# Spreading a kernel's indirect transfers: one lookup or redirection fewer in passes that also gather source rows

## The reference, cut to what matters

```
h  = relu(x @ W_self0 + mean(x[src] by dst) @ W_neigh0 + b0)
h  = h @ W_self1 + mean(h[src] by dst) @ W_neigh1 + b1
x1 = layernorm(x + h)
q = x1@Wq+bq;  k = x1@Wk+bk;  v = x1@Wv+bv;  e = edge_attr@We+be      (4 heads of 128)
alpha = q[dst].(k[src]+e) / sqrt(128);  attn = softmax of alpha by dst
out = sum by dst of (v[src]+e)*attn + x1@Wskip+bskip
z   = elu(layernorm(out) @ Wlin + blin + x1)
result = layernorm(x1 + z)
```

## Time and profile before

| | us |
|---|---|
| median of three runs | 1648.03 |
| profiled execution, its own time | 1646.39 |
| its span | 1644.6 |
| node stage, windows 41 to 650 | 609.0, PE busy 576.5, DVE 595.0, ACT 565.3, POOL 489.9 |
| first sampling stage, windows 650 to 812 | 162.0, PE busy 145.8, DVE 96.6, ACT 59.9, POOL 84.4 |
| second sampling stage, windows 812 to 965 | 153.0, PE busy 141.1, POOL 98.2 |
| edge stage, windows 965 to 1645 | 680.0, PE busy 614.8 |

### The profile page before, as it was taken

One profiled execution on the slowest core, in us unless ns is written; L12 is line 12 of the kernel. 1 busy time (PEld: TensorE's weight loads), 2 busy tenths in 40 slices (PEclk: granted clock), 3 DMA queues, 4 the chain that ended last, 5 costly groups with the idle time before them and its releaser, 6 DMA issues. The chain is left out here.

```text
span 1644.6 us, 33984 instructions
## 1 busy us (share of the span) xinstructions
PE 1495.9 (91%) x7847; PEld 1041.7 (63%) x7847; DVE 1292.1 (79%) x6158; ACT 1179.7 (72%) x3174; POOL 1030.3 (63%) x1038
## 2 busy tenths in 40 slices
PE   4999999999999997999699967999999999999972
PEld 3777777777777775888566643555555555555541
DVE  5999999999999998666468754777777777777762
ACT  2999999999999997344257742777777777777772
POOL 2888888868888884676167627455565555565320
PEclk9999999999999999999899989999999999999996
DMA  2567666644444443233179853333333333333210
GB/s 78 143 161 158 157 159 159 158 149 147 147 147 149 147 147 110 73 94 94 48 225 291 283 180 96 82 82 90 88 90 88 89 88 84 88 89 90 62 37 5
DMA packets 156184, 199.53 MB, mean 121 GB/s; under 512 B 36159, under 2 KB 79342, under 8 KB 156070
## 3 DMA queue, kind: packets, MB, share of 16 engines
q1 hardware_dynamic: 127450, 160.43, 32.4%
q0 software_dynamic: 27200, 36.26, 10.2%
q10 hardware_dynamic: 1420, 1.60, 0.3%
HBM read 106.66 MB, written 100.07 MB: 126 GB/s over the span
## 5 line engine op out<-in xcount | busy, mean ns | idle before, releaser
L1377 POOL DMA_INDIRECT big<-x_tab,look x196 | 199.5, 1018 | 91.7 <-issue 36.9
L1394 POOL DMA_INDIRECT out_dram<-big,idx x98 | 99.8, 1018 | 223.2 <-PE pb L1432 147.8
L737 PE MATMUL pb<-MG_s,big 128*128 128x256 f32 x832 | 207.4, 392 | 26.5 <-ACT big L770 26.4
L737 PEld LDWEIGHTS pb<-MG_s,big 128*128 128x128 f32 x832 | 149.5, 189 | 128.5 <-ACT big L770 112.3
L746 ACT ACTIVATE big<-big 128x128 f32<-128x128 f32 x416 | 180.3, 482 | 0.0
L1611 DVE CUSTOM_DVE_ANT_0 big<-pb,big,zero 128x128 f32<-128x128 f32 x392 | 120.2, 347 | 69.5 <-PE pb L1470 69.3
L719 PE MATMUL pb<-C_s,big 128*128 128x128 f32 x832 | 161.4, 276 | 0.0
L720 PE MATMUL pb<-Ws1c_s,big 128*128 128x128 f32 x832 | 161.3, 276 | 0.0
L868 POOL TENSOR_TENSOR big<-big,cl 128x512 f32<-128x512 f32 x104 | 133.7, 1285 | 36.7 <-DVE big L842 35.7
L1108 POOL DMA_INDIRECT big<-h1e_tab,hidx x98 | 98.2, 1002 | 75.0 <-POOLq L1829 34.1
L1481 PEld LDWEIGHTS pb<-Wg_s,big 128*128 128x128 f32 x784 | 103.1, 192 | 47.3 <-issue 43.8
(11 more groups left out here) (354 smaller groups left out, 4003.1 us busy)
## 6 DMA issues: line engine op xcount, KB each, us to landing
big<-in_x_dram SPq DMA_DIRECT2D x104, 256.0 KB
x_tab<-big SPq DMA_DIRECT2D x98, 256.0 KB
out_dram<-big SPq DMA_DIRECT2D x98, 256.0 KB, 2.2
c_ve<-ve_tab SPq DMA_DIRECT2D x98, 256.0 KB, 2.8
ve_tab<-c_ve SPq DMA_DIRECT2D x66, 256.0 KB
h1e_tab<-a_rows SPq DMA_DIRECT2D x25, 256.0 KB, 2.6
x_tab<-a_rows SPq DMA_DIRECT2D x25, 256.0 KB, 3.7
big<-in_edge_attr_dram SPq DMA_DIRECT2D x97, 64.0 KB
```

The costliest lines, as they stand in the source:

```text
L737: t = pe.matmul(o, b_x1T[:, r * P:(r + 1) * P], MG_s[:], start=True, stop=True)
L1377: g.indirect_dma_start(out=o, out_offset=None, in_=x1_tab, in_offset=bass.IndirectOffsetOnAxis(ap=look[:, a, j:j + 1], axis=0), bounds_che ...
```

## The change

A pass with a `gather_src` has one slot where the others have two, so every pass that also has a `node_row` issues at most three indirect transfers. The 16 slots given up shift the later ones back. Redirections now end in pass 53 (before: pass 49). The first lookup is at slot `NT` + 3 = 101, in pass 55 (before: slot 104, pass 52). 91 lookups fit up to pass 103. The other seven are issued in the first sampling stage, behind POOL's last `gather_src`, and the waits for the lookups and the four operations that make `hidx` go there with them. `after`, `run_matrices`, `a_pool` and others are only moved in the file, to stand behind `b_pool`; this part of the diff is left out.

```diff
+        LOOK_AT = NT + 3
+        B_LOOKS = 2 * TILES - 4 * R - LOOK_AT
+        assert 0 < B_LOOKS < NT and TILES >= 6 * 4 * R
+
+        def look_up(g, e):
+
+            g.indirect_dma_start(out=look[:, 0, e:e + 1], out_offset=None, in_=redirect,
+                                 in_offset=bass.IndirectOffsetOnAxis(ap=idx[:, SRC, e:e + 1], axis=0),
+                                 bounds_check=N - 1, oob_is_err=False).then_inc(dma_k[e % 4], 16)
...
-                if it % 6 == 5 and it < 96:
+                brings = it % 6 == 5 and it < 6 * 4 * R
+                if brings:
                     gather_src(g, it // 6 // R, it // 6 % R)
-                for t in range(2 * it, 2 * it + 2):
+                slot = 2 * it - min(it // 6, 4 * R)
+                for t in range(slot, slot + (1 if brings else 2)):
                     if t < NT:
                         redirect_rows(idx[:, REP, t:t + 1], idx[:, EID, t:t + 1], t % 4)
                     elif t == NT:
                         redirect_rows(split_i[:], tail_i[:, 1:2], t % 4)
-                    elif t >= TILES and t - TILES < NT:
-                        if t == TILES:
+                    elif t >= LOOK_AT:
+                        if t == LOOK_AT:
                             for k in range(4):
                                 g.wait_ge(dma_p[k], 16 * len(range(k, NT + 1, 4)))
...
+                        look_up(g, t - LOOK_AT)
             g.wait_ge(s_row, 16 * (TILES // 8 + (1 if spread < E else 0)))
...
+        def a_pool(g):
+            for s in range(4, NG):
+                after(g, "a_pmT", s - 4)
+                for r in range(min(R, NT - R * s)):
+                    gather_src(g, s, r)
+            for e in range(B_LOOKS, NT):
+                look_up(g, e)
             for k in range(4):
                 g.wait_ge(dma_k[k], 16 * len(range(k, NT, 4)))
             g.tensor_scalar(hf[:, 0, 0:NT], look[:, 0, 0:NT], float(N), float(FAR), ALU.is_lt,
```

More of the change, by code:

```diff
@@ L995, in a_pool @@
                     gather_src(g, s, r)
+            for e in range(B_LOOKS, NT):
+                look_up(g, e)
+            for k in range(4):
+                g.wait_ge(dma_k[k], 16 * len(range(k, NT, 4)))
+            g.tensor_scalar(hf[:, 0, 0:NT], look[:, 0, 0:NT], float(N), float(FAR), ALU.is_lt,
+                            ALU.mult).then_inc(s_look, 1)
+            g.tensor_scalar(hf[:, 1, 0:NT], look[:, 0, 0:NT], float(-N), None, ALU.add).then_inc(s_look, 1)
+            g.wait_ge(s_look, 2)
+            g.tensor_tensor(hf[:, 1, 0:NT], hf[:, 0, 0:NT], hf[:, 1, 0:NT], ALU.add).then_inc(s_look, 1)
+            g.wait_ge(s_look, 3)
+            g.tensor_copy(hidx[:, 0:NT], hf[:, 1, 0:NT]).then_inc(s_look, 1)
+            g.wait_ge(s_look, 4)
         def a_dve(v):
```

## The result

The changed kernel takes 1637.28 us, the median of five runs (1634.38 to 1638.90), against 1648.03 (1645.60 to 1649.31, five runs). The ratio is 0.9935, 95% interval 0.9920 to 0.9949. Forecast were 1637.7 us and a ratio of 0.9937. In a later run (`after_again`) it came to 1637.47 us and 0.9943 (0.9929 to 0.9956).

The account below looks back on a forecast made before the run. In 16 node-stage passes, POOL's late x1c was taken to hold DVE's clip, delaying ACT and PE. Removing this gains 10.3 us, the other parts cost 0: 1648.03 - 10.3 = 1637.7 us, range 1635.9 to 1640.3.

Parts of the forecast that it names:

- The overlap: Node stage: DVE's clip L817 can't run while POOL's late x1c runs; removing all 16 cases gains 10.3 us.
- Rival B: Node stage: the row gather itself disturbs DVE, or stalls only move to other passes; nothing changes, 1648.0 us; chance 4%.
- The tight passes with `dst_row`: Node stage, such as pass 48: x1c would end 0.10 us before the clip's place, so the overlap goes.
- Rival A: Passes loading `dst_row` pay part of the overlap again, 2.4 up to 5.8 us; 1640 to 1643.5 us; chance 7%.
- three slots: Pass 47 before the change: POOL's three slots start at 320.34, 321.67 and 323.30, ahead of `dst_row` and a late x1c.
- The seven lookups and the four operations in the first sampling stage: Behind POOL's last gather, done by about 793 with some 19 us margin; cost nothing.
- rival C: Second sampling stage waits for `hidx`; slower only from 29 us of POOL delay, with 34 us 1653 us; chance 2%.
- D: First sampling stage: the four operations hold DVE on its path, up to 2.5 us, giving 1640.2 us; chance 5%.
- its 0: First sampling stage: cost taken for the four operations possibly holding DVE, given 3.8 us to spare; upper bound 2.5 us.
- Cost nothing: End of the node stage: lookups moved to passes 101 to 103 are an ordinary load of two slots, costing 0.

Follow-up runs that it names:

- e1: The kernel before with DVE's clip moved 1.07 us later in the pass, four indirect transfers kept: 1636.62 us, ratio 0.9929.
- e3: The changed kernel with a 128x1408 memset on POOL at the end of each gathering pass, where the fourth transfer was: 1644.06 us, ratio 0.9983.
- e7: The changed kernel with a 128x512 memset ahead of x1c in passes with `dst_row`, on another chip: 1698.02 us, ratio 0.9976.
- e8: The changed kernel with 11 instead of 7 lookups in the first sampling stage, none in passes 102 and 103: 1632.70 us, ratio 0.9921.
- e2: The kernel before with only the seven lookups, their wait and the four operations moved, two slots in every pass: 1643.16 us, ratio 0.9969.
- e9: e8 with x1c also taken out of pass 103: 1632.50 us, ratio 0.9917.

## Why the prediction was right

**The overlap and its size.** Forecast were 10.2 to 10.4 us in the passes, taken as 10.3; measured are 10.15 in passes 5 to 103. e1 shows the cause with POOL untouched, e3 brings the loss back without a transfer, e7 makes a part of it to measure. Rival B (the gather itself) has fallen with the changed kernel and with e1: both gather in the same passes and have no long one.

**The tight passes with `dst_row`.** 0.10 us forecast, 0.08 found in pass 48, 0.08 to 0.09 in the four such passes. Rival A did not come. (Of the "three slots" that the prediction counts in pass 47 the first is the gather.)

**The seven lookups and the four operations in the first sampling stage.** Done by 793 less the shift, forecast; 782.0, found. Rivals C and D did not come: 20.7 us are left, and DVE's operation beside them kept its 0.60 us. Two readings of the prediction are off here without moving its 0. PE's L1076 does not read what L1016 wrote; it writes the bank that L1016 has read, which gives the same 3.8 us of slack. And rival C calls 34 us twice what the work takes, while by the prediction's own times (778.60 to 793) it is 14.4.

The rule of the Trainium skill ("SBUF — State Buffer", "Who interferes with whom") by which POOL and DVE shut each other out holds for x1c and the clip (1.24 us for 0.15, done at 326.24 where x1c ends at 326.20). It also works the other way: in the kernel before, POOL's cast met DVE's L833, an operation with two inputs, and by the times it waited for it:

```profile
648.18 0.66 DVE L833 SCALAR_TENSOR_TENSOR big<-big 128x512 f32<-128x512 f32 x1
```

The cast, from 648.17, took 0.80 us, to 648.97, 0.13 after L833's end. It takes 0.27 in the kernel after and in e1, where the two do not start together. But the traces do not bear the rule out for every pair. In pass 103 of the kernel before, the clip runs from 646.78 in 0.15 us, all of it inside POOL's L916, a tensor_scalar of 128x98 that had started at 646.44:

```profile
646.44 0.61 POOL L916 TENSOR_SCALAR hf<-look 128x98 f32<-128x98 int32 x1
```

It was not held. In the kernel after, DVE's L957 ran beside L999 with no loss (0.60 against 0.59), while POOL's L1001, which started during L957, took 0.57 us instead of the 0.49 it takes alone in e8.

**The step that was wrong,** though it hardly moved the sum: "In the node stage the four operations ran in its drain and shortened nothing", and with it "Cost nothing" for the lookups moved to passes 101 to 103. The end of POOL's last instruction plus 7.6 us of drain was what the end of the stage waited for, though SP's last store was issued later. Taking the four operations away is worth 3.35 us (e2: 12.16 to 8.81; 0.53 of it is the cast held by DVE, and without that hold the tail of e1, with the same four operations, is 11.61). The lookups that took their place in pass 103 cost 3.1 again (11.93). The two cancel to 0.23 us, which is why 10.3 held: in this part the prediction was lucky. It gave no row for the tail being hidden. The waits of SP's own queue have the sign of it: 4.3 us at the end of the node stage in the kernel before, behind the last landing. That the medians meet the forecast to 0.4 us is luck too, since the five runs spread over 4.5 us; the 10.15 in the passes is not.

## What to carry to other kernels

A tiny instruction can be a pass's bottleneck when another engine shuts it out: look for a line whose longest duration is many times its median, and ask what ends with it. Then there are two cures, and e1 shows that here they are worth the same (564.76 and 564.46 us for the passes): make the long operation earlier (fewer issues ahead of it) or put the short one where the other never runs. At the end of a stage, ask of each engine when it arrives at the meeting point, drain included, not when its last instruction ends; in this kernel, work that is to fill slack should not be POOL's in the last two passes (e8, 2.8 us).

## What the runs showed of the hardware

POOL's DRAIN at the end of a block ends long after POOL's last instruction. At the end of the node stage it is 7.7 us before, 7.6 after, 7.3 in e8 and e9 and 7.0 in e2; at the ends of the three later stages, before and after, it is 6.8 to 8.9 us. At the end of both sampling stages it is hidden, since SP arrives later. At the end of the edge stage it is not: in the kernel before POOL's last instruction ends at 1630.08 and its drain at 1638.93, the others had drained by 1628.4, and all go on at 1639.2. No run here takes work from POOL there. The drains of ACT and DVE end 0.03 to 0.05 us after their last instruction, and SP's takes 7 ns in the row of the kernel after. What POOL's waits for is not shown by any run here; it is somewhat shorter behind an x1c (e2, e8, e9) than behind a lookup or the four operations.

Where POOL's x1c holds DVE's clip, it does so to its end: in all 16 cases before, 16 of e3 and 12 of e7 the clip ends 0.03 to 0.05 us after x1c. POOL's addition L919 does the same in e1. POOL's tensor_scalar L916 does not (0.15 us, before), nor does the issue of an indirect transfer: in pass 48 of the kernel after, `node_row` starts 0.08 us behind the start of the clip and the clip takes 0.16 us.
